# Adapter units of the first layer: residual transposed into the up banks and added to there, loads in another order

## The chip, the cores and the metric

One core of a Trainium2 chip runs the whole kernel. The metric is the device time of one execution in microseconds (us); lower is better. Engines: PE (TensorE), DVE (VectorE), ACT (ScalarE), POOL (GpSimd), and SP (SyncE), which issues nearly all DMAs.

## What the kernel computes

Four sequences of 512 tokens with 512 features, in float32. A block of attention and two MLPs gives `x`; then three adapter layers follow, each with its own weights, chosen for each sequence by an expert number:

```python
x = clip(x + cms_out + modifier, 0, 1)        # y0, the end of the attention and MLP block
# three adapter layers:
residual = x
h = gelu(x @ W_down[e] + b_down[e])           # 512 -> 256
h = h @ W_up[e] + b_up[e]                     # 256 -> 512
h = residual + h
x = layernorm(h) * g[e] + b[e]
```

## The kernel before

**Precision.** A float32 product is made of three matmuls of split numbers: each operand has a high part (rounded by ACT) and a low part (the rest, by DVE or POOL). `mm3` issues high x high, high x low, low x high, and adds them in a bank of PSUM. One 128x512 bank has 512 float32 values on each partition.

**Before the adapters.** The MLPs end with products whose weights stream through a ring of six buffers (`load_operand`); the last six groups of products are added up by DVE (`down_product_add(ci, k)`, k from 0 to 6, two additions of 128x512 each, signalled by `e_done`, and `first_sum_add`, signalled by `f_done`). The result is y0, clipped. Its first pair of sequences was made earlier and lies in memory, once whole (`y0_dram`) and once split (`y0_split`); the second pair stays in `res`. y0 has features on the partitions.

**Units.** A unit `u` is one layer of one sequence: u = 4 x layer + sequence, 12 units. Each needs down weights (`wd[u % 2]`, 1 MB split), up weights (`wu[u % 2]`, 1 MB), two rows of factors (`bc`), and columns (`pp`). On PE the program is a pipeline of steps s: down projection of unit s (`t_down_mm`, 24 matmuls), transposes of unit s - 3 (`t_transpose`, 16), up projection of unit s - 1 (`t_up_mm`, 24). The down projection gives features on partitions, as gelu and the next product want it. The up projection gives tokens on partitions, as the statistics of the layer norm want it: four tiles `UP[0..3]`, banks 0 to 3. After an up projection `z_stats` on DVE adds the residual (which empties the bank, `t_z`) and takes statistics; ACT normalises (`z_norm`); `t_transpose` turns the result back, for the next layer's input, into banks 2 and 3 (d = 0, 1) and two down banks; ACT (`y_split`) and DVE (`y_less_high`, `t_yf`) read these and leave the banks.

**The residual of the first layer** has features on partitions and is needed with tokens there. `y0_to_rows(b)` transposes it (16 transposes of 128x128) into the UP banks, and `y0_rows(b)` on DVE adds the up bias row `bup0` and writes `res` back (`t_res_done`). For this the UP banks are used once more between two up projections: unit 0's residual ahead of down projection 0, unit 1's between down 0 and down 1, those of units 2 and 3 after the up projections of units 0 and 1, the last tile inside the next down projection. Waits of this stage: down projection 0 and 1 wait for `e_done` of the additions k = 5 and k = 6, for `s_yTin` (split y0 landed) and `t_wd` (down weights landed).

**Loads.** SP issues in program order and a wait holds everything behind it. At the end of the MLPs stand: last ring loads with y0's split parts and wd of unit 0 among them; residual 0 (`res[:, 0]`); the last two split parts; a wait for `f_done` 3; residual 1; `unit_down(1)`; `unit_up(0)`; `unit_up(1)`; the rows of two units; then, for u from 2 on, `unit_down(u)` (waits until the down projection u - 2 is over, as it takes its buffer) and `unit_up(u)`.

Of the kernel before, what the change touches and what calls it, by code (L numbers as in the profile page):

```python
# [8 lines left out]
ALU = mybir.AluOpType  # L9
# [3 lines left out]
P = 128  # L13
B = 4
# [126 lines left out]
def build(nc, wqk, wts, xin, bias_in, codes_in, experts_in, up_w, dn_w, dn_p, wdu_all, pp_all, gb_all,  # L141
          bup_all, out):
    ctx = ExitStack()
    with ctx:
# [193 lines left out]
        t_bup0 = sem("first_up_bias_landed")  # L338
        t_rows_full = sem("y0_rows_full")
        t_res_done = sem("y0_residual_done")  # L340
        t_y0hi = sem("y0_hi_done")
# [115 lines left out]
        def _(sp):  # L457
# [232 lines left out]
            for r in range(PREPARED + RING, TOTAL):  # L690
                load_operand(r)
                if r in (PREPARED + COPS, PREPARED + 2 * COPS):
                    x_late_in((r - PREPARED) // COPS - 1)
                bup_at = r - PREPARED - 3 * COPS - 2
                if bup_at % 3 == 0 and 0 <= bup_at < 3 * B:
                    b = bup_at // 3
                    sp.wait_ge(x_added, 2)
                    sp.dma_start(bup0[:, b, :], bup_all[bass.ds(ex[b], 1)].to_broadcast([P, V])).then_inc(t_bup0, 16)
                at_ = r - last_up - RING
                if at_ in YT_AT:  # L700
                    split_rows(*divmod(YT_AT.index(at_), 4))
                if at_ in WD_AT:
                    unit_down_part(0, WD_AT.index(at_))
            sp.wait_ge(s_spill, 16 * 4)
            sp.wait_ge(aop_used, dop_at(NCH - 1, 9) + 1)
            sp.dma_start(res[:, 0, :, :], y0_dram[:, 0]).then_inc(s_y0in[0], 16)
            for k in range(len(YT_AT) - 4, 4):
                split_rows(1, k)
            sp.wait_ge(aop_used, dop_at(NCH - 1, 11) + 1)
            sp.wait_ge(f_done, 3)  # L710
            sp.dma_start(res[:, 1, :, :], y0_dram[:, 1]).then_inc(s_y0in[1], 16)
            unit_down(1)
            unit_up(0)
            unit_up(1)
# [30 lines left out]
        def _(pe):  # L745
# [199 lines left out]

            def y0_to_rows(b, tiles=range(DT)):

                if b < 2:
                    pe.wait_ge(s_y0in[b], 16)
                else:  # L950
                    pe.wait_ge(y0_done, DT * b)
                for i in tiles:
                    if b == 0:
                        pe.wait_ge(e_done, e_count(NCH - 1, 1, i - 2) if i >= 2 else e_count(NCH - 1, 4, i))
                    if b == 1:
                        pe.wait_ge(t_res_done, i + 1)
                    if b > 1:
                        pe.wait_ge(t_z, (b - 2) * DT + i + 1)
                    for d in range(DT):
                        ins = nc.tensor.transpose(UP[i][:, d * P:(d + 1) * P],  # L960
                                                  res[:, b, d, i * P:(i + 1) * P], ident[:, :])
                    ins.then_inc(t_rows_full, 1)

            def t_down_mm(u, b):
                pe.wait_ge(t_wd[u % 2], 16 * (u // 2 + 2))
                for m in range(MT):
# [16 lines left out]
                    ins.then_inc(t_down, 1)  # L983
                    if m == 0 and u in (2, 3):
                        y0_to_rows(u, (DT - 1,))

            def t_up_mm(u, b):
                pe.wait_ge(t_wu[u % 2], 16 * (u // 2 + 1))
                for i in range(DT):
                    if u < 3:  # L990
                        pe.wait_ge(t_res_done, (u + 1) * DT + i + 1)
                    else:
                        pe.wait_ge(t_z, (u - 1) * DT + i + 1)
                    if 2 <= u < 11 and i >= 2:
                        pe.wait_ge(t_yf, (u - 2) * DT + i - 1)
                    for k in range(MT):
                        if i == 0:
                            pe.wait_ge(t_hlo, u * MT + (k + 1))
                        ins = mm3(UP[i], lambda e: h_hl[b % 2][:, e, k, i * P:(i + 1) * P],
                                  lambda e: wu[b % 2][:, e, k, :], k == 0, k == MT - 1)  # L1000
                    ins.then_inc(t_up, 1)

            def t_transpose(u, b):
                for d in range(DT):
                    if u == 11:
                        pe.wait_ge(t_z, 12 * DT)
                    elif u == 10:
                        pe.wait_ge(t_yf, 9 * DT + d + 1)
                    elif u == 9:
                        pe.wait_ge(t_hf, 10 * MT + d + 1)  # L1010
                        if d < 2:
                            pe.wait_ge(t_yf, 8 * DT + d + 3)
                    elif d >= 2:
                        pe.wait_ge(t_hf, (u + 2) * MT + d - 1)
                    elif u:
                        pe.wait_ge(t_z, (u + 1) * DT + d + 3)
                    else:
                        pe.wait_ge(t_res_done, 3 * DT + d + 3)
                    for i in range(DT) if u < 11 else LAST_COLS:
# [5 lines left out]

            y0_to_rows(0)
            for s in range(15):
                if s < 12:
                    t_down_mm(s, s % B)
                if s == 0:  # L1030
                    y0_to_rows(1)
                if 3 <= s:
                    t_transpose(s - 3, (s - 3) % B)
                if 1 <= s < 13:
                    t_up_mm(s - 1, (s - 1) % B)
                if 1 <= s < 3:
                    y0_to_rows(s + 1, range(DT - 1))

# [355 lines left out]
        def _(dve):  # L1394
# [420 lines left out]

            def y0_rows(b):

                dve.wait_ge(t_bup0, 16 * B)

                if b >= 2:  # L1820
                    dve.wait_ge(t_y0lo, (b - 1) * DT)
                dve.wait_ge(t_rows_full, (b + 1) * DT)
                for i in range(DT):
                    nc.vector.tensor_tensor(res[:, b, i, :], UP[i], bup0[:, b, :], ALU.add).then_inc(t_res_done, 1)

            def factors(u, k, n):
# [9 lines left out]
            def z_stats(u, between=None):  # L1836

                for i in range(DT + 2):
                    if i < DT:
# [3 lines left out]
                        if u >= 3:  # L1843
                            if u < 11:
                                dve.wait_ge(t_rmul, (u - 3) * DT + i + 1)
                            dve.wait_ge(t_tr, (u - 2) * DT)
                        nc.vector.tensor_tensor(z[u % 3][:, i, :], UP[i], res[:, u % B, i, :], ALU.add).then_inc(t_z, 1)
                    if 1 <= i < DT + 1:
# [75 lines left out]
            down_product_add(NCH - 1, 6)  # L1924
            y0_rows(0)
            for s in range(12):
# [4 lines left out]
                if s == 0:  # L1931
                    second_pair_y0(0)
                    second_pair_y0(1)
                    h_lo(0, 0)
                    h_lo(0, 1)
                    y0_rows(1)
                if s == 11:
                    h_lo(11, 0)
                    h_lo(11, 1)
                if 1 <= s:  # L1940
                    z_stats(s - 1, None if s == 11 else lambda m: h_lo(s, m))
                if 1 <= s < 3:
                    y0_rows(s + 1)
            last_unit()
# [129 lines left out]
```

## Time and profile before

| what | value |
|---|---|
| median of 3 runs | 1181.37 us (1179.77 to 1182.26) |
| the profiled execution | 1180.58 us, its span 1178.7 us |
| granted clock of TensorE, mean | 0.998 |
| PE busy | 1167.0 us |
| DVE busy | 761.7 us |
| ACT busy | 531.5 us |
| POOL busy | 162.3 us |
| adapters, from the first down projection | from 1012.21 us to the end |

The span goes from the first to the last instruction of the profiled execution; the time of a run also has what lies around it. PE's busy time is the time in which a matmul is under way. The granted clock is a share of TensorE's full speed. All times of the trace count from the span's start.

### The profile page before, as it was taken

To read this page: it belongs to the slowest core of one execution; us is meant where nothing else is said; L and a number is where in the kernel's file an instruction comes from. 1 tells how busy PE (TensorE), PEld (TensorE's weight loads), DVE (VectorE), ACT (ScalarE), POOL (GpSimd) and SP (SyncE) were. 2 spreads that over 40 slices of the span, in tenths; PEclk is the share of its full clock that TensorE was granted. 3 is DMA by queue.
4 is the path that set the end of the run, shared out by engine and by line. 5 is a ranking of instruction groups with operands and counts; after the bars stand their busy time and mean duration, and the time that the engine had idled before them with its cause. 6 is when DMAs were issued, how large, how long until landed. Compare 5 with 4: busy or idle time off the path is not lost.

```text
span 1178.7 us, 15577 instructions
## 1 busy us (share of the span) xinstructions
PE 1167.0 (99%) x5276; PEld 965.8 (82%) x5276; DVE 761.7 (65%) x1352; ACT 531.5 (45%) x965; POOL 162.3 (14%) x146
## 2 busy tenths in 40 slices
PE   9999999999999999999999999999999999999997
PEld 8878888878888788888888888888888888788886
DVE  6345386776767865656567676785555646777786
ACT  5434354564544534343435535433131313347887
POOL 1332130000000000000000000000000000349981
PEclk9999999999999999999999999999999999999999
DMA  5754543536644726263699789756777679946645
GB/s 209 265 208 166 181 176 119 179 136 231 211 159 176 259 100 245 104 234 124 233 406 313 234 295 309 212 188 193 230 192 231 192 230 298 342 144 218 224 166 197
DMA packets 113045, 251.25 MB, mean 213 GB/s; under 512 B 13364, under 2 KB 13364, under 8 KB 109638
## 3 DMA queue, kind: packets, MB, share of 16 engines
q1 hardware_dynamic: 112822, 249.99, 62.6%
q8 instruction: 43, 0.70, 0.2%
q14 instruction: 36, 0.29, 0.1%
q10 hardware_dynamic: 144, 0.26, 0.1%
HBM read 154.78 MB, written 95.43 MB: 212 GB/s over the span
## 4 chain that ended last, share of the span: by engine, by line
PE 89%; DVE 5%; DMA 3%; ACT 2%; issue 1%; POOL 1%; SPq 0%; DVEq 0%; ACTq 0%
PE psum L749 85%; DMA prep<-wdu_dram 2%; PE psum L1022 2%; POOL prep L1965 1%; DMA wd<-wdu_split 1%; DVE c_op L1631 1%; PE psum L803 1%; ACT prep L1062 0%; ACT res L1366 0%; PE psum L798 0%; PE psum L814 0%; DVE dg L1679 0%; DVE ring L1521 0%; DVE res L1703 0%; PE psum L783 0%
## 5 line engine op out<-in xcount | busy, mean ns | idle before, releaser
L749 PE MATMUL psum<-a_op,ring 128*128 128x512 f32 x1344 | 316.5, 389 | 0.3 <-DVE w_t L1563 0.3
L749 PEld LDWEIGHTS psum<-a_op,ring 128*128 128x128 f32 x1344 | 252.1, 188 | 53.2 <-DVE w_t L1563 0.8
L749 PE MATMUL psum<-g_hl,w_hl 128*128 128x512 f32 x1152 | 263.6, 389 | 0.4 <-DVE w_hl L1582 0.4
L749 PEld LDWEIGHTS psum<-g_hl,w_hl 128*128 128x128 f32 x1152 | 216.1, 188 | 46.0 <-DVE w_hl L1582 0.8
L749 PE MATMUL psum<-c_op,ring 128*128 128x512 f32 x672 | 163.3, 390 | 0.4 <-DVE c_op L1631 0.3
L749 PEld LDWEIGHTS psum<-c_op,ring 128*128 128x128 f32 x672 | 125.8, 188 | 27.8 <-DVE c_op L1631 1.8
L1178 ACT ACTIVATE g<-g,sm 128x512 f32<-128x512 f32 x96 | 69.5, 724 | 137.4 <-DVE g L1569 66.7
L1589 DVE TENSOR_TENSOR g_hl<-g,g_hl 128x512 fp32r<-128x512 f32 x96 | 66.1, 689 | 52.0 <-ACT g_hl L1201 51.1
L1158 ACT CAST ring<-asum 128x256 fp32r<-128x256 f32 x96 | 38.5, 404 | 104.3 <-PE psum L749 76.1
L1971 POOL MEMSET acc_u<- 128x1024 f32 x1 | 1.0, 955 | 592.4 <-DVE w_hl L1582 592.4
L1201 ACT CAST g_hl<-g 128x512 fp32r<-128x512 f32 x96 | 58.5, 618 | 53.2 <-PE psum L749 53.2
L749 PE MATMUL psum<-dg,ring 128*128 128x512 f32 x336 | 76.8, 389 | 0.0
L749 PEld LDWEIGHTS psum<-dg,ring 128*128 128x128 f32 x336 | 63.1, 188 | 13.1
L749 PE MATMUL psum<-yT,wd 128*128 128x512 f32 x288 | 68.4, 392 | 0.8 <-DMA wd<-wdu_split 0.8
L749 PE MATMUL psum<-wu,h_hl 128*128 128x512 f32 x288 | 68.4, 393 | 0.0
L1965 POOL TENSOR_TENSOR prep<-prep 128x512 f32<-128x512 f32 x36 | 50.4, 1407 | 128.6 <-ACT prep L1062 128.6
L749 PEld LDWEIGHTS psum<-yT,wd 128*128 128x128 f32 x288 | 53.6, 188 | 12.1 <-DMA wd<-wdu_split 1.1
L749 PEld LDWEIGHTS psum<-wu,h_hl 128*128 128x128 f32 x288 | 53.3, 188 | 10.7
L1602 DVE TENSOR_TENSOR res<-psum,res 128x512 f32<-128x512 f32 x72 | 48.6, 690 | 17.0 <-PE psum L749 17.0
L1185 ACT COPY u_t<-psum 128x512 f32<-128x512 f32 x32 | 18.7, 585 | 89.6 <-PE psum L749 89.6
L1521 DVE TENSOR_TENSOR ring<-asum,ring 128x256 fp32r<-128x256 f32 x96 | 40.1, 420 | 26.4 <-ACT ring L1158 25.8
L1557 DVE TENSOR_TENSOR v_t<-psum,u_t 128x512 f32<-128x512 f32 x32 | 22.1, 690 | 50.1 <-PE psum L749 50.0
(156 smaller groups left out, 1589.4 us busy)
## 6 DMA issues: line engine op xcount, KB each, us to landing
up_operands<-ring SPq DMA_DIRECT2D x168, 256.0 KB, 2.6
ring<-up_operands SPq DMA_DIRECT2D x168, 256.0 KB, 3.0
wdu_split<-prep SPq DMA_DIRECT2D x36, 512.0 KB, 2.9
down_operands<-stage SPq DMA_DIRECT2D x56, 256.0 KB, 4.9
ring<-down_operands SPq DMA_DIRECT2D x56, 256.0 KB, 3.0
rawp<-up_w_dram SPq DMA_DIRECT2D x24, 512.0 KB, 4.9
wraw<-dn_w_dram SPq DMA_DIRECT2D x48, 256.0 KB, 3.9
wu<-wdu_split SPq DMA_DIRECT2D x12, 1024.0 KB, 5.4
```

The lines of the kernel that those rows point to most:

```text
L749: ins = nc.tensor.matmul(ps, lw(el), rw(er), start=first and i == 0, stop=last and i == 2, skip_group_check=skip)
L803: nc.tensor.matmul(bank[HIGH + m], wqT[:, el, k, m * P:(m + 1) * P], wkT[:, er, k, :], start=False, stop=False)
L1022: ins = nc.tensor.transpose(tr_bank(u, d)[:, i * P:(i + 1) * P], z[u % 3][:, i, d * P:(d + 1) * P], ident[:, :])
L1158: nc.scalar.copy(aop_dst(n)[:, 0, :], aop_src(n)).then_inc(aop_hi, 1)
L1178: nc.scalar.activation(dst, src, ACT.Gelu, bias=(cb1, mb1)[l][:, t:t + 1]).then_inc(gelu_done, 1)
L1185: nc.scalar.copy(u_t[:, :], bank[4 * q + BANK_OF[P1]]).then_inc(u_done, 1)
L1201: nc.scalar.copy(g_hl[t % GHL][:, 0, :], g[:, q, 2 * row + seq, :]).then_inc(g_hi_done, 1)
L1521: nc.vector.tensor_tensor(aop_dst(n)[:, 1, :], aop_src(n), f(aop_dst(n)[:, 0, :]), ALU.subtract).then_inc(aop_lo, 1)
L1557: nc.vector.tensor_tensor(v_t[:, :], bank[4 * q + BANK_OF[P6]], u_t[:, :], ALU.add).then_inc(comb, 1)
L1589: nc.vector.tensor_tensor(g_hl[t % GHL][:, 1, :], g[:, q, 2 * row + seq, :], f(g_hl[t % GHL][:, 0, :]), ALU.subtract).then_inc(g_lo_done, 1)
L1602: nc.vector.tensor_tensor(dst, bank[4 * seq + m], dst, ALU.add).then_inc(d_evac, 1)
L1965: nc.gpsimd.tensor_tensor(prep[i][:, 1, :], prep[i][:, 1, :], prep[i][:, 0, :], ALU.subtract).then_inc(p_lo, 1)
```

## The change

The residual of a first-layer unit is transposed into the UP banks immediately ahead of its up projection (`y0_transposed`, called from `t_up_mm`), and the up projection adds on what lies there: its first matmul no longer opens the bank. `y0_rows` and its two semaphores go. `z_stats` adds the bias row `bup0` for the first four units, and the residual as before for the others. For units 2 and 3 the tiles 2 and 3 now wait for `t_yf` before they are transposed. In SP's order the last split parts and `unit_down(1)` come ahead of residual 0, and `unit_up(0)` ahead of residual 1 with its wait for `f_done`.

```diff
--- before.py
+++ after.py
@@ -336,8 +336,6 @@
         t_pp = sem("unit_columns_landed")
         t_bc = [sem(f"unit_rows_landed_{i}") for i in range(2)]
         t_bup0 = sem("first_up_bias_landed")
-        t_rows_full = sem("y0_rows_full")
-        t_res_done = sem("y0_residual_done")
         t_y0hi = sem("y0_hi_done")
         t_y0lo = sem("y0_lo_done")
         t_yhi = sem("y_hi_done")
@@ -701,16 +699,16 @@
                     split_rows(*divmod(YT_AT.index(at_), 4))
                 if at_ in WD_AT:
                     unit_down_part(0, WD_AT.index(at_))
+            for k in range(len(YT_AT) - 4, 4):
+                split_rows(1, k)
+            unit_down(1)
             sp.wait_ge(s_spill, 16 * 4)
             sp.wait_ge(aop_used, dop_at(NCH - 1, 9) + 1)
             sp.dma_start(res[:, 0, :, :], y0_dram[:, 0]).then_inc(s_y0in[0], 16)
-            for k in range(len(YT_AT) - 4, 4):
-                split_rows(1, k)
+            unit_up(0)
             sp.wait_ge(aop_used, dop_at(NCH - 1, 11) + 1)
             sp.wait_ge(f_done, 3)
             sp.dma_start(res[:, 1, :, :], y0_dram[:, 1]).then_inc(s_y0in[1], 16)
-            unit_down(1)
-            unit_up(0)
             unit_up(1)
             sp.wait_ge(aop_used, TOTAL)
             unit_rows(0, 0, 0)
@@ -943,23 +941,22 @@
                 else:
                     down_products(ci)
 
-            def y0_to_rows(b, tiles=range(DT)):
+            def y0_transposed(b):
 
                 if b < 2:
                     pe.wait_ge(s_y0in[b], 16)
                 else:
                     pe.wait_ge(y0_done, DT * b)
-                for i in tiles:
+                for i in range(DT):
                     if b == 0:
                         pe.wait_ge(e_done, e_count(NCH - 1, 1, i - 2) if i >= 2 else e_count(NCH - 1, 4, i))
-                    if b == 1:
-                        pe.wait_ge(t_res_done, i + 1)
-                    if b > 1:
-                        pe.wait_ge(t_z, (b - 2) * DT + i + 1)
+                    else:
+                        pe.wait_ge(t_z, (b - 1) * DT + i + 1)
+                    if b >= 2 and i >= 2:
+                        pe.wait_ge(t_yf, (b - 2) * DT + i - 1)
                     for d in range(DT):
-                        ins = nc.tensor.transpose(UP[i][:, d * P:(d + 1) * P],
-                                                  res[:, b, d, i * P:(i + 1) * P], ident[:, :])
-                    ins.then_inc(t_rows_full, 1)
+                        nc.tensor.matmul(UP[i][:, d * P:(d + 1) * P], res[:, b, d, i * P:(i + 1) * P], ident[:, :],
+                                         start=d == 0, stop=False, is_transpose=True, skip_group_check=True)
 
             def t_down_mm(u, b):
                 pe.wait_ge(t_wd[u % 2], 16 * (u // 2 + 2))
@@ -981,23 +978,21 @@
                         ins = mm3(down_bank(u, m), lambda e: wd[b % 2][:, e, k, m * P:(m + 1) * P],
                                   lambda e: yT[b][:, e, k, :], k == 0, k == DT - 1)
                     ins.then_inc(t_down, 1)
-                    if m == 0 and u in (2, 3):
-                        y0_to_rows(u, (DT - 1,))
 
             def t_up_mm(u, b):
+                if u < B:
+                    y0_transposed(b)
                 pe.wait_ge(t_wu[u % 2], 16 * (u // 2 + 1))
                 for i in range(DT):
-                    if u < 3:
-                        pe.wait_ge(t_res_done, (u + 1) * DT + i + 1)
-                    else:
+                    if u >= B:
                         pe.wait_ge(t_z, (u - 1) * DT + i + 1)
-                    if 2 <= u < 11 and i >= 2:
+                    if B <= u < 11 and i >= 2:
                         pe.wait_ge(t_yf, (u - 2) * DT + i - 1)
                     for k in range(MT):
                         if i == 0:
                             pe.wait_ge(t_hlo, u * MT + (k + 1))
                         ins = mm3(UP[i], lambda e: h_hl[b % 2][:, e, k, i * P:(i + 1) * P],
-                                  lambda e: wu[b % 2][:, e, k, :], k == 0, k == MT - 1)
+                                  lambda e: wu[b % 2][:, e, k, :], u >= B and k == 0, k == MT - 1, skip=u < B)
                     ins.then_inc(t_up, 1)
 
             def t_transpose(u, b):
@@ -1012,10 +1007,8 @@
                             pe.wait_ge(t_yf, 8 * DT + d + 3)
                     elif d >= 2:
                         pe.wait_ge(t_hf, (u + 2) * MT + d - 1)
-                    elif u:
+                    else:
                         pe.wait_ge(t_z, (u + 1) * DT + d + 3)
-                    else:
-                        pe.wait_ge(t_res_done, 3 * DT + d + 3)
                     for i in range(DT) if u < 11 else LAST_COLS:
                         if d == 0:
                             pe.wait_ge(t_zn, u * DT + i + 1)
@@ -1023,18 +1016,13 @@
                                                   z[u % 3][:, i, d * P:(d + 1) * P], ident[:, :])
                     ins.then_inc(t_tr, 1)
 
-            y0_to_rows(0)
             for s in range(15):
                 if s < 12:
                     t_down_mm(s, s % B)
-                if s == 0:
-                    y0_to_rows(1)
                 if 3 <= s:
                     t_transpose(s - 3, (s - 3) % B)
                 if 1 <= s < 13:
                     t_up_mm(s - 1, (s - 1) % B)
-                if 1 <= s < 3:
-                    y0_to_rows(s + 1, range(DT - 1))
 
 
         @block.scalar
@@ -1813,16 +1801,6 @@
                     down_add(ci, 0)
                     down_add(ci, 1)
 
-            def y0_rows(b):
-
-                dve.wait_ge(t_bup0, 16 * B)
-
-                if b >= 2:
-                    dve.wait_ge(t_y0lo, (b - 1) * DT)
-                dve.wait_ge(t_rows_full, (b + 1) * DT)
-                for i in range(DT):
-                    nc.vector.tensor_tensor(res[:, b, i, :], UP[i], bup0[:, b, :], ALU.add).then_inc(t_res_done, 1)
-
             def factors(u, k, n):
 
                 dve.wait_ge(t_rstd, nmr_count(u, k))
@@ -1835,6 +1813,8 @@
 
             def z_stats(u, between=None):
 
+                if u == 0:
+                    dve.wait_ge(t_bup0, 16 * B)
                 for i in range(DT + 2):
                     if i < DT:
                         dve.wait_ge(t_up, u * DT + i + 1)
@@ -1844,7 +1824,8 @@
                             if u < 11:
                                 dve.wait_ge(t_rmul, (u - 3) * DT + i + 1)
                             dve.wait_ge(t_tr, (u - 2) * DT)
-                        nc.vector.tensor_tensor(z[u % 3][:, i, :], UP[i], res[:, u % B, i, :], ALU.add).then_inc(t_z, 1)
+                        rest = bup0[:, u, :] if u < B else res[:, u % B, i, :]
+                        nc.vector.tensor_tensor(z[u % 3][:, i, :], UP[i], rest, ALU.add).then_inc(t_z, 1)
                     if 1 <= i < DT + 1:
                         k = i - 1
                         dve.wait_ge(t_z, u * DT + k + 1)
@@ -1922,7 +1903,6 @@
                                                    op0=ALU.mult, op1=ALU.subtract).then_inc(t_yf, 1)
 
             down_product_add(NCH - 1, 6)
-            y0_rows(0)
             for s in range(12):
                 if 3 <= s < 11:
                     y_less_high(s - 3)
@@ -1933,14 +1913,11 @@
                     second_pair_y0(1)
                     h_lo(0, 0)
                     h_lo(0, 1)
-                    y0_rows(1)
                 if s == 11:
                     h_lo(11, 0)
                     h_lo(11, 1)
                 if 1 <= s:
                     z_stats(s - 1, None if s == 11 else lambda m: h_lo(s, m))
-                if 1 <= s < 3:
-                    y0_rows(s + 1)
             last_unit()
```

## Rows read from the trace of the kernel before

**Rows 1.** The head of the page: PE's busy time and share of the span, matmuls and weight loads.
```profile
PE 1167.0 (99%) x5276; PEld 965.8 (82%) x5276; DVE 761.7 (65%) x1352; ACT 531.5 (45%) x965; POOL 162.3 (14%) x146
```

**Rows 2.** The chain that ended last, in order of time: start us, us, what.
```profile
1013.74 7.09 DMA wd<-wdu_split
...
1052.36 1.75 PE psum L1022 x16
...
1079.43 10.93 PE psum L749 x48
```

**Rows 3.** Timeline of PE, 1002 to 1054: start us, us, engine, line, operation.
```profile
1002.72 7.64 PE L749 MATMUL psum<-dg,ring 128*128 128x512 f32 x33
1010.49 1.97 PE L960 MATMUL psum<-ident,res 128*128 128x128 f32 x16
1012.21 5.73 PE L749 MATMUL psum<-yT,wd 128*128 128x512 f32 x24
1018.08 1.97 PE L960 MATMUL psum<-ident,res 128*128 128x128 f32 x16
1020.88 5.74 PE L749 MATMUL psum<-yT,wd 128*128 128x512 f32 x24 [0.83 <-DMA wd<-wdu_split]
...
1033.14 3.02 PE L749 MATMUL psum<-yT,wd 128*128 128x512 f32 x12
...
1053.87 5.73 PE L749 MATMUL psum<-wu,h_hl 128*128 128x512 f32 x24
```

**Rows 4.** Groups by form, 1010.4 to 1054: the additions of y0_rows.
```profile
L1824 DVE TENSOR_TENSOR res<-psum,bup 128x512 f32<-128x512 f32 x16 | 9.9, 681 | 2.3 <-PE psum L960 2.3
```

**Rows 5.** Timeline of DVE: the sixth addition of the last chunk.
```profile
1010.16 1.29 DVE L1703 TENSOR_TENSOR res<-psum,res 128x512 f32<-128x512 f32 x2
```

**Rows 6.** Timeline of SP, 985 to 1060: issues of loads.
```profile
1002.23 0.32 SPq L528 DMA_DIRECT2D ring<-down_operands  x1
1005.00 0.32 SPq L706 DMA_DIRECT2D res<-y_spill  x1
1005.41 0.86 SPq L641 DMA_DIRECT2D yT<-y_split  x2
1012.65 0.32 SPq L711 DMA_DIRECT2D res<-y_spill  x1
...
1019.59 0.63 SPq L659 DMA_DIRECT2D wd<-wdu_split  x1
```

**Rows 7.** Issues at 1002.23, 1005.9, 1012.65 and 1019.59: KB, us to landing.
```profile
ring<-down_operands SPq DMA_DIRECT2D x1, 256.0 KB, 5.7
yT<-y_split SPq DMA_DIRECT2D x1, 512.0 KB, 7.5
res<-y_spill SPq DMA_DIRECT2D x1, 1024.0 KB, 5.4
wd<-wdu_split SPq DMA_DIRECT2D x1, 1024.0 KB, 13.5
```

**Rows 8.** Windows: busy us of each engine, then PE clock, DMA share, GB/s.
```profile
1012.00:1014.00 2.00, 2.00 (x13) 1.70 (x11) 1.87 (x4) 0.00 (x0) 0.00 (x0) 1.00 0.30 84
1014.00:1016.00 2.00, 2.00 (x11) 1.64 (x10) 2.00 (x4) 0.69 (x1) 0.00 (x0) 1.00 0.87 295
...
1020.00:1022.00 2.00, 1.17 (x6) 0.94 (x6) 2.00 (x4) 2.00 (x5) 1.71 (x2) 1.00 1.05 408
```

**Rows 9.** Timeline of POOL, 1018 to 1036.
```profile
1020.29 10.14 POOL L1976 TENSOR_TENSOR yT<-res,yT 128x512 fp32r<-128x512 f32 x8 [246.24 <-ACT yT L1326]
```

**Rows 10.** Timeline, 1064 to 1067: the transposes of unit 1's result.
```profile
1064.88 1.91 PE L1022 MATMUL psum<-ident,z 128*128 128x128 f32 x16
...
1066.47 2.76 DVE L1921 SCALAR_TENSOR_TENSOR yf<-psum,unit_columns,yT 128x512 f32<-128x512 f32 x4 [2.46 <-ACT yT L1354]
```

**Rows 11.** PE's last instructions in the timeline, and a window after them.
```profile
1171.49 0.98 PE L1022 MATMUL psum<-ident,z 128*128 128x128 f32 x7 [0.31 <-ACT z L1331]
...
1174.00:1176.00 2.00, 0.00 (x0) 0.00 (x0) 0.56 (x1) 0.60 (x2) 0.00 (x0) 0.50 1.00 381
```

## The prediction

> **What bounds the kernel now.** I read the page's head first: PE is busy for 1167.0 us, 99% of the span of 1178.7 [rows 1], so only time in which PE waits, or work taken off PE, can shorten the kernel. The profiled execution took 1180.58 us (span 1178.7 and 1.9 around it), 0.8 us under the median of 1181.37; the sum is made against 1180.58 and its difference carried over to the median. Then the chain in order of time: from 1054.11 us it is PE without a break, in the steady pattern of 48 matmuls in 10.93 us and 16 transposes in 1.75 [rows 2]. One matmul is thus worth 10.93/48 = 0.2277 us there and 0.2275 over several such pieces, one transpose 1.75/16 = 0.109. Before that the chain runs through a DMA: the second unit's down weights, issued last at 1013.74, landed 7.09 us later, and PE started on them at 1020.88 [rows 2, 3].
>
> So I counted PE's slots from the last matmul of the MLP to the third up projection [rows 3]. The MLP's last 33 matmuls start at 1002.72 and end at 1002.72 + 33 x 0.2275 = 1010.23; the up projection of unit 2 starts at 1053.87. These 43.64 us hold 6 x 24 = 144 matmuls (32.76) and 64 + 16 = 80 transposes (8.75), 41.51 us of work. The gaps are therefore 2.1 us: 0.26 ahead of the first transposes (1010.49, the residual's landing); from 1012.21 + 24 x 0.2275 = 1017.67 to 1020.88 less 1.75 of transposes = 1.5, in two waits (residual 1 at 1018.08, weights at 1020.88); 0.4 in small ones. **That is all that any reordering here can win.**
>
> **The change, part by part.** *Transposes.* Their number stays 64 and their shape is the same; they only go to the place right ahead of the up projection of their unit. The price is 0.109 each before and after, so nothing. That the following matmuls add on a bank (start off) instead of opening it has no row of its own, but the second to twelfth matmul into each bank already adds: I take nothing.
>
> *VectorE.* The 16 additions of y0_rows go, 9.9 us [rows 4], and z_stats adds the bias row in place of the residual with the same 128x512 form. They were beside PE's work but for small waits inside the 0.4 us above, which I count as won.
>
> *Head.* The first transposes covered PE while VectorE finished the MLP's adds. Now down projection 0 comes first, and it waits for e_done of the sixth addition: the first of the pair that starts at 1010.16 and takes 1.29 us together is done about 0.65 to 0.69 later [rows 5], so PE starts at about 1010.88. New gap 0.65 in place of 0.26. Then down 0 (5.46), down 1 (5.46), 16 transposes (1.75), up 0 (5.46): down projection 2 is due at 1010.88 + 18.13 = **1029.0**. Before, it began at 1033.14 [rows 3]. It is due 4.1 us earlier, and what it waits for has to come earlier too.
>
> *Loads.* SyncE's order after its last ring load (1002.23 [rows 6]) was residual 0 at 1005.00, two pieces of y0's split, residual 1 at 1012.65 (held by VectorE's f_done), both halves of wd1, wu0, wu1, four rows of factors, and wd2 at 1019.59. Now the split, wd1, residual 0 and wu0 are issued by about 1006, before the wait for f_done; behind it stand residual 1, wu1, the four rows and wd2. That cures the wait for wd1. But wd2, the reload of the first weight buffer, stays last in the queue. Before, it landed at 1019.59 + 13.5 = 1033.1 [rows 6, 7], exactly when it was needed, and it is what I follow.
> All these pass one DMA queue, one after the other. After the last ring load (1002.23 + 5.7 = 1007.9) two MB, residual 0 and the two pieces of y0, took until 1013.4 (the second piece's issue near 1005.9 [rows 6], and 7.5): 2.75 us a MB. Residual 1 landed at 1012.65 + 5.4 = 1018.05, and the five MB from wd1 to wd2 took from there to 1033.1, 15.05 us. In the new order the same eight MB follow on the ring load without a pause: 1007.9 + 3 x 2.75 + 15.05 = **1031.2**. The saving against 1033.1 is the pause of the queue, which the stretch from 1012 to 1014 us shows: 84 GB/s there [rows 8]. Bounds: filling the pause at 390 GB/s (84 missing from 2 us, and 295 from the next 2) gives (306 x 2 + 95 x 2)/390 = 2.1 us, so 1031.0; if one slow DMA engine sets the landings, it stood still only from 1013.4 to about 1014.3, so 1032.2.
> PE thus waits 1031.2 - 1029.0 = 2.2 us at the head of down projection 2 (2.0 to 3.2). Nothing is behind it on PE but work that it needs anyway, and everything else of unit 2 is ready: GpSimd made eight parts in 10.14 us from 1020.29 [rows 9], here from about 1019, and the unit needs the first four. The other moved loads are early: wd1 lands near 1013.4 for 1016.3, residual 0 and wu0 by 1018.9 for 1021.8 and 1023.5, wu1 by 1024.4 for 1036.
>
> *Steps 3 and 4.* Residual 2 and 3 are now transposed after t_transpose, and their tiles 2 and 3 wait for VectorE to leave the same banks (t_yf). In a later step the transposes start at 1064.88 and VectorE's parts at 1066.47, four in 2.76 [rows 10]: two are done at 1067.85, while the group for tile 3 would start at 1064.88 + 1.75 + 12 x 0.109 = 1067.94. Margin 0.1 us; I take nothing, bounds 0 and 0.2 for both steps.
>
> **Sum.** Gaps before 2.1; after 0.65 + 2.2 = 2.85; difference +0.7 us (with the bounds of the landing +0.5 to +1.7). 1180.58 + 0.7 = 1181.3 for the profiled time; on the median 1181.37 + 0.7 = **1182.1 us**. From 1054 us to the end nothing changes but the shift.
>
> **The rivals.**
> (B) The transfers keep up and the wait is hidden. For it: the queue reached 408 GB/s from 1020 to 1022 [rows 8]; eight MB (8.39 million bytes) at that rate after 1007.9 land at 1028.5, before 1029.0. Against it: the five MB above took 15.05 us, 348 GB/s by landings. Then the gaps are 0.65 and the kernel takes 1181.37 - 1.5 = 1179.9.
> (C) The wait for wd2 grows and the kernel is slower beyond noise. If the queue makes no more of its early start than the slow case and the rows' broadcasts, which land late, delay it further, it lands as before, at 1033.1: wait 4.1, +2.6, 1184.0. It decides from a landing at about 1032.9. For it: its landing was the slowest of all, 13.5 us, with the queue at full load for 13 us already, and now for 20. Against it: the pause of about 2 us is there to be filled.
> The Trainium skill (DMA: Bandwidth & Descriptors, "Where 436 GB/s comes from") names some 358 GB/s as the memory's limit for a core. The trace's 408 GB/s does not agree; by the rule, the 8.39 million bytes would take 23.4 us in place of 21.5 at 390, an estimate that puts wd2 1.9 us later, at this rival.
> (D) PE's clock falls at the new gap or in the doubled run of transposes. The granted clock is 1.00 (2.4 GHz) all through the gap of 1.1 us before 1020.88, and 0.50 (1.2 GHz) at 1174 us, after sparse transposes and some 1.5 us of idling [rows 11]. Here the gap is twice as long as the one that left it alone, but stands in dense work. If down projection 2 ran at half clock, 24 x 0.2275 = 5.5 us are added: 1187.5.
> The Trainium skill (TensorE: Matmul & The Clock Gate, "Part 4: PE-mode transpose") says that transposes do not count as activity for the clock; the blocks of 16 here kept 1.00, and no stretch before has 32 of them in a row.
> (E) The loads and adds of this stage are all hidden and nothing changes: excluded on the head, whose gap is in the chain.
>
> **How the numbers follow.** Forecast 0.54; B 0.26; C 0.13; D 0.05; others 0.02. A measurement of this kernel can tell about 0.2% (2.4 us) from no change: its three runs spread over 2.5. Forecast and B lie within that, with noise carrying some of B over on the fast side; C and D lie at or above it: faster 0.10, same 0.73, slower 0.17. The most that could be won is 1.5 to 2.1 us, so a clear gain needs noise or something I don't see. Range 1179.3 to 1184.5: B less half a microsecond of noise, C plus half. The forecast's own is 1181.3 to 1183.3.
>
> **What would show it.** Right: PE goes from the MLP's last matmul to down projection 0 with a gap near 0.65; no gap ahead of down 1; a gap of 2.2 us released by DMA wd<-wdu_split ahead of down 2, near 1029 to 1031; wd2 issued near 1017.5 and landing near 1031; 16 fewer VectorE additions; t_transpose and residual transposes back to back; from there the old pattern. Wrong: no gap at down 2 (B), a gap over 4 us (C), 0.50 in the granted clock after it (D), a transpose dearer than 0.109 us, or a VectorE wait between the third and fourth group of residual transposes in steps 3 and 4.

## The result, and the profile after

Over the runs that were timed together the changed kernel took 1184.08 us (median), the kernel before 1180.13: ratio 1.0032, 95% interval 1.0025 to 1.0039. It is slower, by 3.9 us where 0.7 was forecast. One of its fifteen executions took 4202 us and is left out of these numbers. The profiled execution took 1184.29 us; its span is 1182.5 us, 3.8 more than before.

Where PE waited, the first lines of the list of waits of the changed kernel (engine, what it runs <- what it waited for: us in total, times, longest):

```profile
PE psum L747 <- DMA wd<-wdu_split: 2.7, 1, 2.7
PE psum L747 <- DVE pT L1388: 1.9, 1, 1.9
```

The first is the predicted wait. PE's timeline shows it (start us, us, engine, line, operation, count, idle before and its releaser):

```profile
993.08 19.20 PE L747 MATMUL psum<-dg,ring 128*128 128x512 f32 x84
1012.88 11.17 PE L747 MATMUL psum<-yT,wd 128*128 128x512 f32 x48 [0.60 <-issue]
1023.88 1.91 PE L958 MATMUL psum<-ident,res 128*128 128x128 f32 x16
1025.55 5.70 PE L747 MATMUL psum<-wu,h_hl 128*128 128x512 f32 x24
1033.92 5.76 PE L747 MATMUL psum<-yT,wd 128*128 128x512 f32 x24 [2.68 <-DMA wd<-wdu_split]
```

The chain that ended last has the two blocks of transposes of step 3 (start us, us, what):

```profile
1052.36 1.75 PE psum L1015 x16
1054.11 1.88 PE psum L958 x16
```

The MLP's last matmul ends at 993.08 + 84 x 0.2275 = 1012.19, 1.96 us later than before's 1010.23 [rows 3]. So one half of the profiled loss lies ahead of the stage that was changed. Behind that point come 1182.5 - 1012.19 = 170.3 us, before 1178.7 - 1010.23 = 168.5: the stage costs 1.8 us. Its parts: 0.7 us at the head, no gap ahead of down 1 (48 matmuls in one piece), 33.92 - 25.55 - 5.46 = 2.9 ahead of down 2, and 0.13 each in steps 3 and 4, where the second block of transposes takes 1.88 against 1.75 for the first. That is 3.9 against 2.1.

The other half is the second wait of the list, in the attention, whose code is the same. In the windows (columns as in [rows 8]) PE pauses from 63.6 to 65.5 us, and behind that its granted clock is at half for about 3.4 us (the shares 0.62 and 0.53 of two windows of 2 us):

```profile
64.00:66.00 2.00, 0.46 (x2) 0.41 (x3) 1.20 (x2) 2.00 (x5) 1.27 (x1) 1.00 0.47 135
66.00:68.00 2.00, 2.00 (x8) 1.51 (x7) 2.00 (x5) 2.00 (x5) 0.00 (x0) 0.62 0.78 262
68.00:70.00 2.00, 2.00 (x6) 1.58 (x5) 2.00 (x4) 1.93 (x4) 0.61 (x1) 0.53 0.35 131
```

Now the loads of the changed kernel, first the issues in SP's timeline, then the landing of the last of them (us from issue), then the queue in windows:

```profile
1007.13 0.83 SPq L707 DMA_DIRECT2D res<-y_spill  x1
1008.14 0.77 SPq L664 DMA_DIRECT2D wu<-wdu_split  x1
1014.59 0.34 SPq L711 DMA_DIRECT2D res<-y_spill  x1
1015.13 0.63 SPq L664 DMA_DIRECT2D wu<-wdu_split  x1
...
1018.76 0.62 SPq L657 DMA_DIRECT2D wd<-wdu_split  x1
```

```profile
wd<-wdu_split SPq DMA_DIRECT2D x1, 1024.0 KB, 15.1
```

```profile
1012.00:1014.00 2.00, 1.40 (x7) 0.98 (x6) 1.92 (x3) 0.00 (x0) 0.00 (x0) 1.00 1.08 419
...
1024.00:1026.00 2.00, 2.00 (x19) 1.96 (x18) 0.00 (x0) 2.00 (x4) 2.00 (x2) 1.00 1.09 354
1026.00:1028.00 2.00, 2.00 (x11) 1.64 (x10) 0.69 (x1) 0.70 (x2) 2.00 (x3) 1.00 1.02 147
1028.00:1030.00 2.00, 2.00 (x11) 1.65 (x10) 1.44 (x3) 0.00 (x0) 2.00 (x3) 1.00 0.96 261
```

The pause of the queue that the prediction meant to fill is filled: 419 GB/s from 1012 to 1014, where before showed 84 [rows 8]. But from 1026 the DMA engines are busy (share 1.02) and move only 147 and then 261 GB/s. In this stretch the four row loads pass: they land from 1025.6 to 1031.3. wd2 lands at 18.76 + 15.1 = 1033.9, which is 21.7 us after the MLP's last matmul; before it was 22.9 [rows 3, 6, 7]. Of the forecast 1.9 us of earlier landing 1.2 came, in this execution.

### The profile page after: what moved, and what is told of

Same layout as the page of the kernel before. It is cut to its first block, busy times and chain, and to the rows that moved or that the text cites. A ratio compares the mean times of both kernels' runs of the same rounds, so it can differ in the third digit from the quotient of the medians.

```text
span 1182.5 us, 15556 instructions
## 1 busy us (share of the span) xinstructions
PE 1167.3 (99%) x5276; PEld 966.5 (82%) x5276; DVE 755.9 (64%) x1336; ACT 531.4 (45%) x965; POOL 162.3 (14%) x146
## 4 chain that ended last, share of the span: by engine, by line
PE 90%; DMA 4%; DVE 3%; ACT 1%; POOL 1%; issue 0%; SPq 0%; DVEq 0%; ACTq 0%
PE psum L747 86%; DMA prep<-wdu_dram 2%; PE psum L1015 2%; DMA wd<-wdu_split 1%; POOL prep L1942 1%; DVE c_op L1619 1%; PE psum L801 1%; PE psum L958 0%; ACT prep L1050 0%; ACT res L1354 0%; PE psum L796 0%; PE psum L812 0%; DVE ring L1509 0%; PE psum L781 0%; DVE pT L1388 0%
```

## The experiments

Times behind the MLP are counted from the end of its last matmul (start of its last piece in the timeline plus its matmuls at 0.2275 us), to keep apart what happens before. "Rest" is the span from there to its end: 168.5 us in before, 170.3 in the profile above.

**The computation alone.** The changed kernel with SP's order of before:

```diff
-            for k in range(len(YT_AT) - 4, 4):
-                split_rows(1, k)
-            unit_down(1)
             sp.wait_ge(s_spill, 16 * 4)
             sp.wait_ge(aop_used, dop_at(NCH - 1, 9) + 1)
             sp.dma_start(res[:, 0, :, :], y0_dram[:, 0]).then_inc(s_y0in[0], 16)
-            unit_up(0)
+            for k in range(len(YT_AT) - 4, 4):
+                split_rows(1, k)
             sp.wait_ge(aop_used, dop_at(NCH - 1, 11) + 1)
             sp.wait_ge(f_done, 3)
             sp.dma_start(res[:, 1, :, :], y0_dram[:, 1]).then_inc(s_y0in[1], 16)
+            unit_down(1)
+            unit_up(0)
             unit_up(1)
```

> The changed kernel with the loads in the order of before. Theory (the loads set the adapters' start): down projection 1 now is due about 5.5 us after down 0 starts, and its weights are issued only behind the wait for f_done, so PE waits some 4.5 us for DMA wd; wd2 then lands just as it is due, no second wait. From the end of the MLP's matmuls to the end of the span about 3.3 us more than in before. Rival (adding on transposed data is dearer by itself): the transposes or the up projections of units 0 to 3 take longer than 1.75 and 5.46 us, and the stage is longer by more than the waits add up to. Second rival (the rest of the loss has nothing to do with this stage): the part of the span before the MLP's last matmul differs from before's by about 1.9 us here too.

Measured: 1186.59 us, ratio 1.0047 (1.0034 to 1.0060). The rest is 174.7 us, 6.2 more than before, where 3.3 was expected. Its timeline and windows of PE:

```profile
1010.42 5.72 PE L747 MATMUL psum<-yT,wd 128*128 128x512 f32 x24 [0.60 <-issue]
1021.00 7.93 PE L747 MATMUL psum<-yT,wd 128*128 128x512 f32 x24 [4.86 <-DMA wd<-wdu_split]
1028.76 1.91 PE L958 MATMUL psum<-ident,res 128*128 128x128 f32 x16
1030.43 5.73 PE L747 MATMUL psum<-wu,h_hl 128*128 128x512 f32 x24
1036.00 5.61 PE L747 MATMUL psum<-yT,wd 128*128 128x512 f32 x24
```

```profile
1020.00:1022.00 2.00, 1.00 (x2) 0.83 (x3) 0.00 (x0) 2.00 (x4) 2.00 (x2) 0.50 1.04 407
1022.00:1024.00 2.00, 2.00 (x6) 1.59 (x5) 0.00 (x0) 0.04 (x1) 2.00 (x3) 0.50 1.05 395
1024.00:1026.00 2.00, 2.00 (x6) 1.55 (x6) 0.00 (x0) 0.00 (x0) 2.00 (x3) 0.58 1.07 381
1026.00:1028.00 2.00, 2.00 (x10) 1.65 (x9) 0.00 (x0) 0.69 (x1) 2.00 (x2) 1.00 1.03 161
1028.00:1030.00 2.00, 2.00 (x17) 1.79 (x16) 0.00 (x0) 1.03 (x2) 0.48 (x1) 1.00 0.81 98
```

The wait for wd1 is the expected one (4.9 for 4.5), and the up projections and the blocks of transposes have their old length. What was not expected is that the 24 matmuls behind the wait take 1028.76 - 1021.00 = 7.8 us in place of 5.5: the granted clock stands at 0.50. A wait of 4.9 us cost 7.2. The part ahead of the MLP's end was not longer here (it ends at 1009.7). And the slow stretch of the queue is here too, with the loads in the order of before: 161 and 98 GB/s, while the four row loads land (1026.6 to 1032.7).

**The loads alone.** The kernel before with SP's order of the changed kernel (the same edit the other way round).

> The kernel before with only the loads in the changed order. Theory (each half of the change needs the other): the first transposes still stand ahead of down projection 0, but residual 0 now lands behind the split parts and wd1, some 6 us after the MLP's last matmul; PE waits there 5 to 6 us in place of 0.3, then nothing for wd1, residual 1 or wd2. Gaps 6.4 against 2.1: 4.3 us slower, and up to 2.3 more if the granted clock falls after the wait, as it did in the run with the computation alone after 4.9 us. Rival (the order of loads is good by itself): within 1 us of before.

Measured: 1186.54 us, ratio 1.0053 (1.0038 to 1.0067). PE's timeline:

```profile
989.91 19.20 PE L749 MATMUL psum<-dg,ring 128*128 128x512 f32 x84
1014.77 3.67 PE L960 MATMUL psum<-ident,res 128*128 128x128 f32 x16 [5.66 <-DMA res<-y_spill]
1018.10 6.79 PE L749 MATMUL psum<-yT,wd 128*128 128x512 f32 x24
1024.73 1.91 PE L960 MATMUL psum<-ident,res 128*128 128x128 f32 x16
```

PE waits 5.7 us for residual 0, and again the half clock comes on top: 16 transposes in 3.3 us and 24 matmuls in 6.6, together 2.7 more than at full clock. The rest is 175.6 us, 7.1 more than before. The row loads land from 1022.8 to 1025.3 here, and the queue keeps its rate until it runs empty, though the loads stand in the changed order:

```profile
1020.00:1022.00 2.00, 2.00 (x10) 1.60 (x8) 2.00 (x6) 0.00 (x0) 0.00 (x0) 0.90 1.05 386
1022.00:1024.00 2.00, 2.00 (x10) 1.69 (x9) 1.72 (x6) 0.69 (x1) 0.00 (x0) 1.00 0.96 350
```

So each half of the change alone costs some 6 us, and both together 2 to 4: the halves are one design, and neither is a gain by itself.

**wd2 ahead of the rows.** The changed kernel with

```diff
             sp.wait_ge(aop_used, TOTAL)
+            unit_down(2)
             unit_rows(0, 0, 0)
             unit_rows(1, 0, 1)
             for u in range(2, 14):
                 if u < 12:
-                    unit_down(u)
+                    if u > 2:
+                        unit_down(u)
                     unit_up(u)
```

> The changed kernel with the reload of the first down buffer (wd2) issued before the four rows of factors. Theory (PE's wait of 2.7 us is for wd2, which stands last, behind the rows): it lands 5 us or more earlier, the wait is gone, only about 0.7 at the head and 0.3 in steps 3 and 4 stay; the part behind the MLP is some 1.2 us shorter than in before and 3 us shorter than in the changed kernel. Rival (the DMA engines are slow there whatever stands in the queue): the wait shrinks by less than 1.5 us, or a wait for wu or for the rows takes its place. If the changed kernel's loss has a part in front of the MLP's end, that part of 1.9 us is still in some of the runs.

Measured: 1178.77 us, ratio to before 0.9984 (0.9975 to 0.9993). Rest 1177.4 - 1010.15 = 167.25, 1.2 less than before, to the tenth what was expected. wd2 landed at 16.78 + 9.7 = 1026.5, needed at 1029.05, and PE goes through:

```profile
1023.51 5.70 PE L749 MATMUL psum<-wu,h_hl 128*128 128x512 f32 x24
1029.05 5.61 PE L749 MATMUL psum<-yT,wd 128*128 128x512 f32 x24
```

```profile
wd<-wdu_split SPq DMA_DIRECT2D x1, 1024.0 KB, 9.7
```

In the stage the whole loss is thus this one wait and what follows from it; the rest of the change is a gain of 1.2 us, over half of the 2.1 that could be had.

**What makes wd2 late.** Two theories: the volume ahead of it, or the rows, which copy one row of 2 KB to 128 partitions. First the rows read from 128 different rows of memory, at the same place:

```diff
+            def unit_rows_plain(u):
+                for i in range(2):
+                    sp.dma_start(bc[u][:, i, :], y0_dram[:, u, i, :]).then_inc(t_bc[u], 16)
...
-            unit_rows(0, 0, 0)
-            unit_rows(1, 0, 1)
+            unit_rows_plain(0)
+            unit_rows_plain(1)
```

> The changed kernel in which the four loads of factor rows of units 0 and 1 (one row of 2 KB copied to 128 partitions each) are replaced by loads of the same size and place from 128 different rows of memory; the factors of two units are thus other numbers, all else is computed. Theory 1 (rows read 128 times over are slow: 113 to 295 GB/s from 1026 to 1033 us in the changed kernel): wd2 lands 2 to 3 us earlier and PE's wait for it is under 1 us. Theory 2 (only the volume ahead of wd2 counts): landing and wait as in the changed kernel, 2.7 us.

Measured: 1179.43 us, ratio 0.9986 (0.9977 to 0.9994). wd2 landed at 15.76 + 12.6 = 1028.4, 18.9 us after the MLP's last matmul, against 21.7 above; PE waited under half a microsecond (down 2 at 1028.39, due at 28.0). Of these 2.8 us, 0.3 is not the loads': counted from the issue of the last ring load, wd2 landed 27.2 us later here and 29.7 in the changed kernel. Theory 1 holds in this kernel: rows of another kind, and the wait is gone.

Then two doses, each executed once: two of the four row loads behind wd2, and wu1 behind wd2 with all rows ahead.

> The changed kernel with two of the four row loads behind wd2. Theory (each row load of 256 KB ahead of wd2 costs it its own slow time, about 1.2 to 1.5 us, where 0.66 would be its share by volume): wd2 lands 2.4 to 3 us earlier than in the changed kernel, near 19.5 us after the MLP's last matmul, and PE's wait shrinks to 0.5 us or less. By volume alone it would land 1.3 us earlier and PE would wait 1.4 to 2.3 us.

> The changed kernel with the up weights of unit 1 (1 MB) issued behind wd2, and all four row loads still ahead of it. Theory (volume counts as well as the rows): one MB less ahead is 2.7 us at the queue's usual rate, so wd2 lands near 19 to 20 us after the MLP's last matmul and PE waits for under 1 us. Rival (only the rows count, because the queue idles behind them): the landing stays near 21.7 to 22.7 and the wait at 2.7 to 3.6.

The landings of wd2 in the two (issued at 1015.92 and 1016.77):

```profile
wd<-wdu_split SPq DMA_DIRECT2D x1, 1024.0 KB, 12.3
```

```profile
wd<-wdu_split SPq DMA_DIRECT2D x1, 1024.0 KB, 14.4
```

Half the rows behind: 1028.2, 18.1 us after the MLP's last matmul, no wait worth naming (0.1); the time was 1178.76, beside 1180.31 of before. That is 3.6 us earlier, but PE waited 0.9 us for VectorE inside the MLP here, so the MLP ended later against the loads. Counted from the issue of the last ring load it is again 27.2 against 29.7: 2.5 us earlier for 0.5 MB less ahead, where volume alone would give 1.3. wu1 behind: 1031.2, 21.0 us after it, a wait of 2.0 us; that is 0.7 us earlier than above for 1 MB less ahead (1.5 to 1.7 than in the two later profiles of the changed kernel, below), where volume would give 2.7. Here theory and rival both miss: the landing moved, but by less than the volume. And the slow stretch of the queue moved with the rows, as the windows of this second kernel show:

```profile
1020.00:1022.00 2.00, 2.00 (x11) 1.60 (x10) 0.00 (x0) 2.00 (x5) 2.00 (x3) 1.00 1.06 281
1022.00:1024.00 2.00, 2.00 (x19) 1.96 (x18) 0.00 (x0) 2.00 (x5) 2.00 (x2) 1.00 1.02 134
1024.00:1026.00 2.00, 2.00 (x11) 1.64 (x10) 0.69 (x1) 0.71 (x2) 2.00 (x3) 1.00 0.96 220
1026.00:1028.00 2.00, 2.00 (x11) 1.65 (x10) 1.43 (x3) 0.00 (x0) 2.00 (x3) 1.00 1.01 384
```

It begins at 1020 to 1022 here and at 1024 to 1026 above, two windows earlier, with one MB less in front; 2.0 us of this is the earlier end of the MLP.

**The same rows in the kernel before.**

> The kernel before with the four loads of factor rows of units 0 and 1 read from 128 different rows of memory in place of one (their factors are other numbers). Theory (one row read for 128 partitions is slow wherever it stands): wd2, which lands 22.9 us after the MLP's last matmul in before, lands 2 us or more earlier; the time behind the MLP stays 168.5 us, because nothing waits for it there. Rival (the rows are slow only in the changed kernel's crowd): it lands at 22.9 as before.

The rival was right. wd2 landed at 18.10 + 13.2 = 1031.3, 22.9 us after the MLP's last matmul (1008.4), as with the real rows (the rest was 168.8 us; PE waited 1.6 us for residual 0, and not for wd1). In before the rows cost nothing, and in the windows of the kernel before (with the real rows) the queue keeps its rate while they pass:

```profile
1024.00:1026.00 2.00, 2.00 (x10) 1.66 (x9) 0.00 (x0) 0.63 (x1) 2.00 (x3) 1.00 1.06 388
...
1028.00:1030.00 2.00, 2.00 (x10) 1.65 (x10) 1.31 (x3) 0.38 (x1) 2.00 (x2) 1.00 1.05 390
```

The order of the loads is not what makes the rows slow. From the first of the four landings to the last it was 3.5 us in the kernel before and 2.5 with its code and the changed order (the loads alone); it was 5.8 in the changed kernel and 6.1 with its code and the old order (the computation alone). Where all four rows stand ahead of wd2, the slow rows thus go with the changed computation. What in it makes them slow is open: no run takes it apart.

**Twice more the changed kernel, once more the kernel before.**

> The changed kernel once more, for a second profile of it and its times on this chip. Theory (the loss has two parts: some 1.9 us of this stage, present always, and some 1.9 us from a wait of PE near 65 us of the attention after which the granted clock falls, present by chance): this profile shows the stage's part again, and the first part either as before or again with the clock at half for some 4 us; the times fall near 1181.9 or 1183.8. Rival (the whole loss belongs to the stage): the part behind the MLP is 3.5 us longer than in before.

> The changed kernel, one more profile. Theory (wd2's landing varies with the slow row loads, between about 21.5 and 23 us after the MLP's end, and the granted clock falls behind the longer waits): a wait of 2.5 to 3.7 us ahead of down 2; with more than 3 us also some 1.5 us for a clock at half. The part in front of the MLP's end may be short or 1.9 us long: if it is chance, it need not be long a third time.

> The kernel before, one more profile, to see how far the part in front of the MLP's end varies by itself. Theory (chance): the wait near 65 us for VectorE's pT differs from the 0.5 us of the first profile in some looks, between 0 and 2 us. Behind the MLP the same 168.5 us as in the first profile, within 0.5.

The changed kernel: 1183.72 us, ratio 1.0021 (1.0012 to 1.0030), and 1186.23 in the single execution. Both profiles have the longer wait, and a fallen clock behind it; the first of them:

```profile
1025.64 5.70 PE L747 MATMUL psum<-wu,h_hl 128*128 128x512 f32 x24
1034.95 7.11 PE L747 MATMUL psum<-yT,wd 128*128 128x512 f32 x24 [3.61 <-DMA wd<-wdu_split]
1041.89 1.91 PE L958 MATMUL psum<-ident,res 128*128 128x128 f32 x16
```

```profile
1034.00:1036.00 2.00, 1.05 (x3) 0.86 (x4) 1.62 (x6) 0.00 (x0) 0.19 (x1) 0.61 1.05 407
1036.00:1038.00 2.00, 2.00 (x7) 1.57 (x6) 0.16 (x1) 0.00 (x0) 1.03 (x1) 0.54 1.05 399
```

24 matmuls take 1041.89 - 1034.95 = 6.9 us, 1.5 more than at full clock; in the other profile the wait is 3.5 and the price 1.7. The rest is 172.6 us in both, 4.1 more than before; the kernel before again had 168.45, with 0.8 us for its wait near 65 us. So the stage costs 1.8 us where the wait stays short, and 4.1 where it is a microsecond longer and the clock falls.

Which of the two is the usual case? The profiled executions with the longer wait took 1186.64 us, the slowest of its twelve, and 1186.23, so 4.1 is rather the upper end. But a fall of the clock is common: the mean granted clock of an execution was 0.997 or less in 23 of 26 timed executions of the changed kernel, in 9 of 46 of the kernel before, and in none of 11 with wd2 ahead of the rows. The mean does not tell where the clock fell.

The part ahead of the MLP's end was long in all three profiles of the changed kernel, but each time elsewhere. In the first it was the attention's wait with the clock behind it. In the second, half of it came there and half near 900 us, where PE waited for a ring load. In the third the attention's wait was 1.2 us (0.5 in before), which an earlier start made up for, and the wait for a ring load was 1.8 us:

```profile
898.78 4.33 PE L747 MATMUL psum<-a_op,ring 128*128 128x512 f32 x18 [1.84 <-DMA ring<-up_operands]
```

The MLP ended at 1012.2, 1012.3 and 1011.8 us in these, and between 1008.4 and 1010.3 in the ten profiles of the other kernels, before's two among them. The expectation said chance; three of three against none of ten is too much for that to be called shown. Timed together, the changed kernel and the one with wd2 ahead of the rows differ by 5.0 us (1183.72 and 1178.77), where the stage of the first profile explains 3.1: the other 1.9 is either this part or the longer wait with its clock, and the times alone can't tell which.

**Residual 0 first.** An attempt at a better version: wd2 ahead of the rows, and the head's gap covered again.

```diff
+            y0_transposed(0)
             for s in range(15):
...
-                if u < B:
+                if 0 < u < B:
                     y0_transposed(b)
```

with residual 0 issued first, then the split parts, wd1 and wu0, all ahead of the wait for f_done.

> The changed kernel with wd2 ahead of the rows, residual 0 ahead of the split parts and wd1, and the transposes of unit 0 before down projection 0, where they cover the additions of VectorE. Theory (the gap of 0.7 us at the head is the wait for the sixth addition, and the transposes of unit 0 hide it): gap 0.3 at the head, no wait for wd1 (due 7.5 us after the MLP's end, landing near 6), none for wd2; the part behind the MLP 1.6 us shorter than before's, 0.4 less than with wd2 moved alone. Rival (wd1 lands too late behind residual 0): a wait ahead of down 1 gives it back.

Measured: 1179.88 us, ratio 0.9992 (0.9983 to 1.0002). In its profile residual 0 is late:

```profile
1011.47 1.97 PE L960 MATMUL psum<-ident,res 128*128 128x128 f32 x16 [1.15 <-DMA res<-y_spill]
1013.19 11.15 PE L749 MATMUL psum<-yT,wd 128*128 128x512 f32 x48
```

The head's gap is 1.15 by the timeline, where it was 0.60 without this edit and should have been cured; rest 167.8; wd1 and wd2 were in time. It is not better than wd2 ahead of the rows alone. I can't separate its first load's lateness from the 0.4 us by which the ring load ahead of it was late too in this profile.

## Why the prediction was right and where it was off

The sign and the mechanism were right, the size was not: +0.7 us forecast, +3.9 measured. That the time still lies inside the stated range is partly luck: in the profile 1.9 us of the loss came from a part of the kernel that the sum left alone. By its own steps:

- *The transposes and adding on them cost nothing.* Right: in all kernels a block of 16 takes its old time, the up projection 5.5.
- *VectorE's additions are off the path.* Right: 16 instructions fewer (1336 for 1352) and no wait of PE for it in steps 1 to 4.
- *Head: 0.65 us for the sixth addition.* Right: 0.7 (0.60 idle by the timeline).
- *The wait for wd1 goes.* Right: down 0 and down 1 are one piece of 48.
- *wd2 lands 1.9 us earlier than before, wait 2.2.* The term that was mis-sized. It landed 1.2, 0.2 and 0.4 us earlier in the three profiles (21.7, 22.7 and 22.5 us after the MLP's last matmul), and PE waited 2.7 to 3.6. The sum took over the 15.05 us that before's five MB needed and counted the pause of the queue as pure gain. The pause was filled, but the row loads, which passed at 384 to 390 GB/s before, now passed at 147 to 265. Plain rows and wd2 ahead of the rows both took the wait away. That the forecast came near the landing of the first profile is partly luck: from the landing of the last ring load (1010.45) the eight MB took 23.4 us there for 23.3 forecast, because the queue was faster than assumed ahead of the rows (392 to 427 GB/s from 1012 to 1020) and slower in them, and the ring load itself landed 0.6 us later after its issue. In the two later profiles the eight MB took 25.1 and 24.3.
- *The clock stays.* Held as rival D with 0.05 and priced at 5.5 us. It happened in two of the three profiles of the changed kernel, at 1.5 and 1.7 us: the low clock lasted about 3.4 us, not through the whole down projection. This is the second half of the miss: where the stage cost 4.1 us, 2.6 are waits and 1.5 the clock. The Trainium skill (TensorE: Matmul & The Clock Gate, "HAM oscillation — how this bites in real kernels") says that work behind a long wait for a load starts at half clock; the rows of the longer waits agree, those of the 2.7 us wait do not show it.
- *Transposes in blocks of 32 might lower the clock* (also D). It did not: 1.00 through steps 3 and 4, as the window shows.

```profile
1052.00:1054.00 2.00, 2.00 (x19) 1.91 (x18) 0.21 (x1) 1.60 (x3) 2.00 (x2) 1.00 1.07 403
1054.00:1056.00 2.00, 2.00 (x19) 1.85 (x17) 2.00 (x4) 2.00 (x4) 2.00 (x3) 1.00 0.28 101
```

- *Steps 3 and 4: nothing, bounds 0 and 0.2.* 0.13 each, 0.26 together.
- *Rival C* (wd2 no earlier than before, 2.6 us slower) described two of three profiles in its landing; its reason, the rows' late landing at full load, is what the experiments bear out in part: the full load alone does not do it, as the kernel before with the changed order shows. It left the clock out.
- The 1.6 to 2 us ahead of the stage had no step: that code is unchanged. It is in all three profiles, at different places.

What stays open: what in the changed computation makes the row loads slow; and whether the part ahead of the MLP's end belongs to the kernel or to chance. The stage alone explains 1.8 to 4.1 of the 3.9 us.

## What to carry to other kernels

When loads are moved to fill a pause of the queue, follow the last transfer that the next stage waits for, not the one whose wait is cured, and don't count the queue's average rate for it: a load that cost nothing in one kernel can be slow in the next, as the rows here, with either order of the loads. Move small loads that nobody needs soon (here rows needed some 15 us later) behind the big one that is needed first: that one edit turned 0.3% slower into 0.16% faster. And add to a wait of PE what the clock took behind waits like it, here 1.5 to 2.7 us.

## What the runs showed of the hardware

- A pause of PE costs more than its length. Behind waits of 4.9 and 5.7 us the granted clock was 0.50 and the next work took 2.3 and 2.7 us more; behind 3.5 and 3.6 us, 1.7 and 1.5 more. It stood at half for about 6.8 us in the first two and 3.4 in the others, by the windows. Length alone does not decide: 2.7 us in dense matmuls left it at 1.00, while 1.9 us in the attention, shortly behind a block of transposes, brought 0.62 and 0.53; 1.4 and 1.2 us at that same place left it at 1.00.
- While loads of one row for 128 partitions landed, the queue moved 98 to 281 GB/s in kernels with the changed computation and all four rows ahead of wd2, with either order of the other loads and the DMA engines' share at 0.8 to 1.1, and 350 to 390 GB/s in kernels with the computation of before, also with either order. With only two of the rows ahead of wd2 it moved 346 to 358, and with loads of 128 different rows in their place 369 to 389, both in the changed computation.
